# Second attention's opening: own projection of batch 0 in two banks, step 1 in the order of the steps without keys, sums of expert results one step later

## The chip, the cores and the metric

One core of a Trainium2 chip. Its engines run in parallel, each its own program in order, and meet only at semaphores: PE (TensorE: matrix products, into the eight banks of PSUM), DVE (VectorE), ACT (ScalarE), POOL (GpSimd) and SP (SyncE, which here issues transfers). The metric is the device time of one execution in microseconds.

## The reference, cut to what matters

Two layers, each an attention to a context and a mixture of experts. What the change touches is the second attention, which starts while the sums of the first mixture's results are still being added to x.

```python
x = x + tanh(g_ffn[0]) * L0_ffn(layernorm(x))          # 8 experts, top 2: the sums of expert results
x = x + tanh(g_xattn[1]) * L1_xattn(layernorm(x), ctx) # the attention of this change

# L1_xattn, per batch (16 batches, 100 rows, 256 columns, 16 heads of 16), context of 361 rows:
q, k, v    = split(x @ Wqkv + bqkv)
_, ka, va  = split(ctx @ Wqkv_aux + bqkv_aux)
h_main = softmax(q @ k.T / 4)  @ v      # own rows
h_aux  = softmax(q @ ka.T / 4) @ va     # context rows
out    = (h_main * (1 - sigmoid(g)) + h_aux * sigmoid(g)) @ Wo + bo
```

## The kernel before

The function `attend1` holds the second attention: five programs, one for each engine, written out in order. They run over steps t from -1 to 19. In step t the batches t+1 (scores for the maxima), t (exponents), t-1 (sums with the values) and t-2 (output) are under way at once, and the projections of batch t+2 are made.

The scores are computed twice. `by_query(b, u)` puts queries on partitions; DVE's `maxima(b, u)` reduces them to row maxima in two halves. `by_key(b, u)` puts keys on partitions, subtracts the maxima by a further product, and ACT's `exponents(b, u)` reads them. The unit u runs over four: two groups of heads by two members, for `by_query`, and four tiles of keys (own rows, three chunks of the context), for `by_key`. PE alternates: `by_query(t+1, u)`, `by_key(t, u)`, u = 0 to 3. All share three pairs of banks (`scores_free`), so that each product waits for the reader of the one before the last: `by_key(t, u)` for the first half of `maxima(t+1, u)`, `by_query(t+1, u+1)` for the first half of `exponents(t, u)`.

All other products of a step go through the last two banks in turn, in the order of the list `ring`, which is built from `ORDER`, or for the steps 12 to 14 from `LIGHT_ORDER` (the last batches' keys are made by then, so these steps have no key projection; they make the values early and order some of their work differently: the sums over the context in two halves around `by_query(t+1, 2)`, `project_own` behind `by_key(t, 2)`, `values_own` ahead of `by_key(t, 3)`, on ACT `exponents(t, 2)` ahead of `take_own`). `into(name, b)` waits until the bank's last content is taken.

`project_own(b)` makes queries and own keys of batch b: eight products into one bank. ACT's `take_own(b)` copies them: four copies of the queries (each group of heads, masked for two members, `qz`), two of the keys (`kT`). `turn_x(b)` transposes the normalized rows that DVE's `normed(b)` writes; `moments(g)` and `newton(g)` make the statistics of a group of batches (group 0: batches 0 and 1, group 1: 2 and 3, then four each), with a power on POOL between them (`root(g)`). `keep_warm(bank, n)` runs n products whose result nobody reads; these fillers stand in step -1 and 0.

The opening: batches 0 and 1 are transposed and projected, then step -1 makes the four `by_query` of batch 0 with the two key projections of batch 4 between them. In step 0 there is nothing to sum yet. In step 1 the values of batch 2 have been made in advance, so that this step makes keys but no values.

`fed` holds the sums of the first mixture's results. SP loads them back (`fed.ways`), DVE adds the first batches at once (`vector_first`) and then three batches of each group of four (`fed.vector(dve, g)`: six instructions, line 2122); the fourth is weighted by ACT (`fed.scalar`, line 2130) and added by POOL (`fed.gpsimd`, line 2104). Group 1's stand ahead of step -1, group 2's in step 0, group 3's at the end of step 1. `moments(g)` waits for the group it needs.

Behind the last of them the semaphores of the first mixture are handed on to the second: DVE, ACT, PE and SP `leave`, POOL clears them (`second.clear`), and the engines `enter` at the start of step 3 (SP: in its step 2, ahead of `prep.load`, which loads the router and the shared expert of the second mixture).

Lines of the profile: 1392 is `by_query`, 1412 and 1418 `by_key`, 1359 a key projection, 1374 `project_own`, 1366 `turn_x`, 1351 `turn_max` (the transposed maxima, for `take_max` on DVE, line 1094), 1346 a filler, 1434 the sums with the values, 1449 values and output. On DVE 1087 and 1088 are `maxima`, 1051 to 1059 `moments`, 1066 to 1072 `newton`, 1077 `normed`; on ACT 1238 and 1240 are `take_own`, 1249 `exponents`.

## Time and profile before

| | us |
|---|---|
| median of 3 runs | 1229.87 (1229.16 to 1230.22) |
| profiled execution | 1233.03 |
| its span | 1231.3 |
| PE busy | 1169.8 (95%), granted clock 0.98 on average |
| DVE, ACT, POOL busy | 595.4, 479.4, 391.7 |
| second attention, from the own projection to by_query(4,0) | 545.88 to 632.36 |

Times within the trace are us from the start of its span. A row of an engine gives start, busy time, engine, line, operation, what it writes and reads, and in brackets how long the engine had been idle and what ended that.
### The profile page before, as it was taken

What the parts mean: (1) busy time and instruction counts of PE and PEld (TensorE: products, weight loads), DVE (VectorE), ACT (ScalarE), POOL (GpSimd) and SP (SyncE); (2) the same over time, 40 slices, a digit from 0 to 9 for tenths busy, and PEclk for the clock granted to TensorE, in tenths of its full rate; (3) what the DMA queues carried; (4) which work ended last, traced back from release to release, by engine and by line L of the source; (5) the groups of instructions that cost most, each with busy time, mean ns of one, the idle gap of its engine ahead of it and who ended that gap; (6) DMA issues with size and microseconds to landing.
All of it is one profiled execution on the core that took longest, in us unless ns stands there. A gap on an engine that the chain in (4) does not pass through costs nothing. (4 is left out here: it accounts for less than half of the span.)

```text
span 1231.3 us, 29193 instructions
## 1 busy us (share of the span) xinstructions
PE 1169.8 (95%) x11425; PEld 901.6 (73%) x11425; DVE 595.4 (48%) x1437; ACT 479.4 (39%) x1130; POOL 391.7 (32%) x411
## 2 busy tenths in 40 slices
PE   6999999977999999998799999999998999999998
PEld 4767777756999999974466666666665579999975
DVE  5777777774210001057566666567656612111226
ACT  3545555523323332324445444444454232233221
POOL 3666666632223222131101011010011245555420
PEclk9999999977999999999899999999999999999999
DMA  6011111305999998640021000000000459999965
GB/s 182 24 28 36 28 37 44 122 15 190 383 325 337 316 341 315 250 135 19 2 87 30 16 21 21 26 9 9 2 9 14 165 196 349 350 360 353 341 224 168
DMA packets 64392, 180.93 MB, mean 147 GB/s; under 512 B 10176, under 2 KB 36608, under 8 KB 55808
## 3 DMA queue, kind: packets, MB, share of 16 engines
q1 hardware_dynamic: 55088, 156.40, 36.9%
q0 software_dynamic: 8064, 22.03, 5.0%
q8 instruction: 92, 1.51, 0.5%
q10 hardware_dynamic: 1104, 0.64, 0.2%
q14 instruction: 44, 0.36, 0.1%
HBM read 163.11 MB, written 15.93 MB: 145 GB/s over the span
## 5 line engine op out<-in xcount | busy, mean ns | idle before, releaser
L2301 ACT ACTIVATE ex_hT<-kept_psum,ex_w 128x128 f32<-128x128 f32 x464 | 132.9, 369 | 294.8 <-PE kept_psum L2356 157.4
L2356 PE MATMUL kept_psum<-ex_xT,ex_w 128*128 128x128 f32 x1856 | 222.5, 276 | 0.0
L2356 PEld LDWEIGHTS kept_psum<-ex_xT,ex_w 128*128 128x128 f32 x1856 | 215.7, 193 | 0.1
L2367 PE MATMUL kept_psum<-ex_w,ex_hT 128*128 128x256 f32 x928 | 214.0, 379 | 0.0
L2263 DVE TENSOR_TENSOR ex_yt<-kept_psum,ex_b 128x256 f32<-128x256 f32 x84 | 35.7, 425 | 353.6 <-PE kept_psum L2367 353.6
L2367 PEld LDWEIGHTS kept_psum<-ex_w,ex_hT 128*128 128x128 f32 x928 | 170.1, 190 | 19.8
L2229 POOL DMA_INDIRECT ex_results<-ex_yt,ex_to_row x84 | 83.0, 988 | 254.9 <-DVE ex_yt L2263 254.9
L1249 ACT ACTIVATE at_probs<-kept_psum 120x800 f32<-120x800 f32 (+2 forms) x128 | 101.3, 842 | 85.5 <-PE kept_psum L1418 85.5
L1088 DVE TENSOR_REDUCE at_negmax<-kept_psum 100x2 f32<-100x722 f32 x128 | 115.5, 902 | 0.0
L568 ACT ACTIVATE at_probs<-kept_psum 120x800 f32<-120x800 f32 (+1 forms) x96 | 80.1, 837 | 73.7 <-PE kept_psum L691 73.6
L410 DVE TENSOR_REDUCE at_negmax<-kept_psum 120x8 bf16<-120x800 f32 (+1 forms) x96 | 90.6, 985 | 23.4 <-PE kept_psum L682 23.0
L329 POOL TENSOR_TENSOR at_sum<-at_probs 120x800 f32<-120x800 f32 (+1 forms) x47 | 76.9, 1635 | 75.1 <-ACT at_probs L568 74.9
L2222 POOL DMA_INDIRECT ex_xt<-ex_normed,ex_from_row x84 | 81.8, 974 | 50.6 <-DVE ex_from_row L1959 25.5
L1779 POOL TENSOR_TENSOR ex_r<-ex_var,kept_mhalf 100x2 f32<-100x2 f32 x16 | 11.3, 705 | 242.1 <-DVE ex_var L1774 242.1
L1087 DVE TENSOR_REDUCE at_negmax<-kept_psum 100x2 f32<-100x200 f32 x128 | 46.4, 363 | 83.6 <-PE kept_psum L1392 83.0
L1392 PE MATMUL kept_psum<-at_kT,at_qz 32*100 32x461 f32 x512 | 68.5, 605 | 5.5 <-ACT at_probs L1249 3.6
L1412 PE MATMUL kept_psum<-at_qz,at_kT 32*120 32x200 f32 (+2 forms) x1024 | 61.5, 354 | 9.7 <-DVE at_negmax L1088 9.2
L1412 PEld LDWEIGHTS kept_psum<-at_qz,at_kT 32*120 32x120 f32 (+2 forms) x1024 | 41.7, 175 | 26.0 <-issue 21.5
L691 PE MATMUL kept_psum<-at_negmax,at_identb 120*120 120x400 bf16 (+1 forms) x192 | 50.7, 347 | 7.6 <-DVE at_negmax L410 7.6
L639 PE MATMUL kept_psum<-at_ctx,at_wk 128*128 128x361 f32 x128 | 48.6, 506 | 7.1 <-DMA at_bk<-in_L_xattn_bk 6.4
L1449 PE MATMUL kept_psum<-at_wkv_aux,at_ctx 128*120 128x256 f32 (+1 forms) x192 | 48.3, 390 | 0.9 <-DVE ex_yt L2263 0.9
L682 PE MATMUL kept_psum<-at_qz,at_kT 32*120 32x200 f32 (+1 forms) x768 | 47.3, 361 | 1.4 <-ACT at_qz L559 0.7
(252 smaller groups left out, 1691.1 us busy)
## 6 DMA issues: line engine op xcount, KB each, us to landing
ex_w<-in_pack_in SPq DMA_DIRECT2D x32, 1028.0 KB
ex_w<-in_pack_out SPq DMA_DIRECT2D x32, 1024.0 KB
ex_w<-in_pack_in SPq DMA_DIRECT2D x52, 514.0 KB
ex_w<-in_pack_out SPq DMA_DIRECT2D x52, 512.0 KB
at_ctx<-in_ctxT SPq DMA_DIRECT2D x31, 361.0 KB, 3.6
ex_normed<-ex_xhat SPq DMA_DIRECT2D x16, 200.0 KB
ex_w<-ex_results SPq DMA_DIRECT2D x6, 400.0 KB
ex_sw<-in_L_ffn_sW SPq DMA_DIRECT2D x2, 1024.0 KB
```

What stands on the lines that cost most here:

```text
L329: pool.tensor_tensor(sum2[0:r, :, :], p[:, :, 0:T2], p[:, :, T2:T], ALU.add).then_inc(sum2_done, 1)
L410: dve.tensor_reduce(negmax[0:r, half, :].rearrange("p (s h) -> p s h", h=HS), by_head, AX, ALU.max, negate=True).then_inc(max_done, 1)
L568: act.activation(probs[t % 2][0:r, j, half * HH:(half + 1) * HH, :].rearrange("p (s h) t -> p s (h t)", s=2), score_pair(t, j, half)[0:r, ...
L1088: dve.tensor_reduce(by_strip[:, :, HS + u], pair[0:T, :, T:KEYS], AX, ALU.max, negate=True).then_inc(max_done, 1)
L1249: act.activation(probs[b % 2][0:r, u, half * HH:(half + 1) * HH, :].rearrange("p (s h) t -> p s (h t)", s=2), score_pair("k", b, u, half)[ ...
L1392: last = pe.matmul(score_pair("q", b, u, strip // 2)[0:T, strip % 2, 0:KEYS], qz[b % NQ][rows, i, a, :], kT[b % NK][rows, i, :], start=Tru ...
L1412: pe.matmul(score_pair("k", b, u, strip // 2)[0:r, strip % 2, i * 2 * T:(i + 1) * 2 * T], kT[b % NK][rows, i, k0:k0 + r], qz[b % NQ][rows, ...
L2222: pool.indirect_dma_start(xt[t % GATHERS][:, :], None, xhd, bass.IndirectOffsetOnAxis(from_row[:, t:t + 1], 0)).then_inc(gathered[t % GATH ...
L2229: pool.indirect_dma_start(ways, bass.IndirectOffsetOnAxis(to_row[:, t:t + 1], 0), yt[t % SCATTERS][:, :], None).then_inc(scattered[t % SCA ...
L2301: last = act.activation(hT[t % N][:, c, :], ps_h[:, (t * U + u) % N, i * P:(i + 1) * P], ACT.Gelu, bias=w1[t % N][:, B1 + c:B1 + c + 1])
L2356: last = pe.matmul(ps_h[:, (t * U + u) % N, i * P:(i + 1) * P], w1[t % N][:, c * ff + f:c * ff + f + P], xT[t % N][:, c, :], start=(c == 0 ...
L2367: last = pe.matmul(ps_y[:, t % N, 0:D], hT[t % N][:, c, :], w2[t % N][:, c * D:(c + 1) * D], start=(c == 0), stop=(c == FC - 1))
```

## The change

- The own projection of batch 0 goes into two banks (`own`, `own_more`), each with one group of heads, queries and keys. ACT's `take_first_own` copies the first bank, waits for its own copies, then the second; `by_query(0, u)` waits for the copy of its own queries only (`first_own_taken`). `project_own(1)` moves behind `by_query(0, 0)`.
- In step -1 the key projections of batch 4 move down by one unit; four fillers stand behind `by_query(0, 3)`, and five new ones behind `turn_max(0)` in step 0.
- Step 1 takes `NO_VALUES_ORDER`: keys as before, and the rest in the order of the steps without keys.
- The DVE sums of group 1 go from ahead of step -1 into step 0, those of group 2 from step 0 into step 1 and those of group 3 from the end of step 1 into step 2, between the first two maxima there. `moments(1)` goes into step 0, `newton(1)` and `normed(2)` behind the second maxima of step 0. POOL makes all its additions ahead of `root(1)`.
- The handover of the semaphores comes one step later on all engines.
- The two buffers `probs` change places, and in the second mixture the tiles `w1` and `b2` move ahead of `shT`.

```diff
...
     mix = m.sb("mix", [T, D])
-    probs = [m.sb(f"probs{i}", [P, UNITS, H, T]) for i in range(2)]
+    probs = [m.sb(f"probs{i}", [P, UNITS, H, T]) for i in (1, 0)][::-1]
     vm = [m.sb(f"vm{i}", [T, H, 32]) for i in range(2)]
...
                    ("turn_aux", -2), ("own", 2), ("mixT", -2), ("value_own", 0), ("out", -2))
-    LIGHT = range(B - NK + 1, B - 1)
+    NO_VALUES_ORDER = (("max", 0), ("key0", 4), ("key1", 4)) + LIGHT_ORDER[3:]
+    LIGHT, NO_VALUES = range(B - NK + 1, B - 1), range(1, 2)
+
+    def order(t):
+        return LIGHT_ORDER if t in LIGHT else NO_VALUES_ORDER if t in NO_VALUES else ORDER
+
+    def spread_out(t):
+        return t in LIGHT or t in NO_VALUES
+
+    first_own_taken = m.sem("first_own_taken")
     ready = {n: m.sem(f"{n}_ready") for n, _ in ORDER}
     taken = {n: m.sem(f"{n}_taken") for n, _ in ORDER}
+    ready["own_more"], taken["own_more"] = m.sem("own_more_ready"), m.sem("own_more_taken")
     x_ready = taken["out"]
...
 
-    opening = [(n, b) for b in range(PRE) for n in ("value01", "value2")] + [(n, b) for n in ("xT", "own") for b in range(2)]
-    ring = opening + [(n, used(n, off, t)) for t in STEPS for n, off in (LIGHT_ORDER if t in LIGHT else ORDER) if used(n, off, t) is not None]
+    opening = [(n, b) for b in range(PRE) for n in ("value01", "value2")] + [("xT", 0), ("xT", 1), ("own", 0), ("own_more", 0), ("own", 1)]
+    ring = opening + [(n, used(n, off, t)) for t in STEPS for n, off in order(t) if used(n, off, t) is not None]
     ring_at = {use: i for i, use in enumerate(ring)}
...
                 early.load_context(sp, t + NC)
-            if t == 2:
+            if t == 3:
                 fed.finished(sp)
...
         root(0)
-        fed.gpsimd(pool, 0)
+        for g in range(NG):
+            fed.gpsimd(pool, g)
         root(1)
-        for g in range(1, NG):
-            fed.gpsimd(pool, g)
         for b in range(B + 4):
-            if b == 2:
+            if b == 3:
                 second.clear(pool)
...
         take_value2(PRE)
-        moments(1)
-        fed.vector(dve, 1)
         for t in STEPS:
...
                 dve.wait_ge(filled, 6 + 2 * NV)
-            if t == 3:
+            if t == 4:
                 second.enter(dve)
...
             if t == 0:
+                moments(1)
+            if t == 1:
+                fed.vector(dve, 2)
+            if t == 2:
+                fed.vector(dve, 3)
+                fed.finished(dve)
+            if on(t + 1):
+                maxima(t + 1, 1)
+            if t == 0:
                 newton(1)
                 normed(2)
-            if on(t + 1):
-                maxima(t + 1, 1)
             if on(t - 2):
...
             if t == 0:
-                fed.vector(dve, 2)
+                fed.vector(dve, 1)
             if t in (1, 2):
...
                 take_value2(t + 1)
-            if t in LIGHT:
+            if spread_out(t):
                 take_value_own(t)
...
                 residual(t - 2)
-            if on(t) and t not in LIGHT:
+            if on(t) and not spread_out(t):
                 take_value_own(t)
-            if t == 1:
-                fed.vector(dve, 3)
-                fed.finished(dve)
+            if t == 2:
                 second.leave(dve)
...
             last.then_inc(taken["own"], 1)
+
+        def take_first_own():
+            act.wait_ge(masks_set, 4)
+            for i, name in enumerate(("own", "own_more")):
+                act.wait_ge(ready[name], 1)
+                bank = ring_bank(name, 0)
+                act.activation(kT[0][:, i, 0:T], bank[:, (KC + i) * T:(KC + i + 1) * T], ACT.Identity, bias=bqk[:, KC + i:KC + i + 1])
+                for a in range(2):
+                    last = act.activation(qz[0][:, i, a, :], bank[:, i * T:(i + 1) * T], ACT.Identity, bias=bqm[:, i, a:a + 1],
+                                          scale=own[:, a:a + 1]).then_inc(first_own_taken, 1)
+                act.wait_ge(first_own_taken, 2 * i + 2)
+                act.sem_inc(taken[name], 1)
 
...
         take_xT(1)
-        take_own(0)
+        take_first_own()
         fed.scalar(act, 1)
...
         for t in STEPS:
-            if t == 3:
+            if t == 4:
                 second.enter(act)
...
                 take_sum(t - 1, 1)
-            if x_batch(t) is not None and t not in LIGHT:
+            if x_batch(t) is not None and not spread_out(t):
                 take_own(x_batch(t))
...
                 exponents(t, 2)
-            if x_batch(t) is not None and t in LIGHT:
+            if x_batch(t) is not None and spread_out(t):
                 take_own(x_batch(t))
-            if t == 3:
+            if t == 4:
                 prep.scale_bias(act)
...
 
+        def project_first_own():
+            pe.wait_ge(taken["xT"], 1)
+            for i, name in enumerate(("own", "own_more")):
+                bank = into(name, 0)
+                for part in (i, KC + i):
+                    for c in range(KC):
+                        last = pe.matmul(bank[:, part * T:(part + 1) * T], w[:, c, part * P:(part + 1) * P], xT[0][:, c, :],
+                                         start=(c == 0), stop=(c == KC - 1))
+                last.then_inc(ready[name], 1)
+
         def by_query(b, u):
             scores_free("q", b, u)
+            if b == 0:
+                pe.wait_ge(first_own_taken, u + 1)
             if u == 0:
-                pe.wait_ge(taken["own"], b + 1)
+                if b > 0:
+                    pe.wait_ge(taken["own"], b + 1)
                 if b < KEYED:
...
         pe.wait_ge(w_loaded, 32)
-        project_own(0)
-        project_own(1)
-        keep_warm(psum[:, 2, :], 2)
+        project_first_own()
         for t in STEPS:
-            if t == 3:
+            if t == 4:
                 second.enter(pe)
...
                 by_query(t + 1, 0)
+            if t == -1:
+                project_own(1)
             if t == 0:
                 turn_max(t)
-            if key_batch(t) is not None:
+                keep_warm(into("xT", 2), 5)
+            if key_batch(t) is not None and t != -1:
                 project_key(key_batch(t), 0)
...
             if t == -1:
-                project_key(key_batch(t), 1)
+                project_key(key_batch(t), 0)
             if on(t - 1):
...
             if on(t - 1):
-                sum_up(t - 1, 1, range(HG // 2 if t in LIGHT else HG))
+                sum_up(t - 1, 1, range(HG // 2 if spread_out(t) else HG))
             if t == 0:
...
                 by_query(t + 1, 2)
-            if t in LIGHT:
+            if spread_out(t):
                 sum_up(t - 1, 1, range(HG // 2, HG))
...
                 prep.early_tensor(pe, range(t - B, t - B + 1))
-            if x_batch(t) is not None and t not in LIGHT:
+            if x_batch(t) is not None and not spread_out(t):
                 project_own(x_batch(t))
...
                 by_key(t, 2)
-            if x_batch(t) is not None and t in LIGHT:
+            if x_batch(t) is not None and spread_out(t):
                 project_own(x_batch(t))
...
             if t == -1:
-                keep_warm(into("max", 0), 3)
+                project_key(key_batch(t), 1)
             if t == 0:
...
                 by_query(t + 1, 3)
+            if t == -1:
+                keep_warm(into("max", 0), 4)
             if t == 0:
...
                 values2(t + 1)
-            if t in LIGHT:
+            if spread_out(t):
                 values_own(t)
...
                 project_out(t - 2)
-            if on(t) and t not in LIGHT:
+            if on(t) and not spread_out(t):
                 values_own(t)
...
             addend = m.sb("addend", [T, GB, D])
+            b2s = m.sb("b2", [P, E, D])[:, :, :]
+            w1 = [m.sb(f"w1_{i}", [P, B1 + FC]) for i in range(N)]
             shT = [m.sb(f"shT{i}", [P, FS, GT]) for i in range(2)]
-            b2s = m.sb("b2", [P, E, D])[:, :, :]
             syT = Pool(nc, "ex1", scaled_at).sb("syT", [P, KC, GT])
...
         yt = [m.sb(f"yt{i}", [P, D]) for i in range(SCATTERS)]
-        w1, w2 = slots("w1_", [P, B1 + FC]), slots("w2_", [P, FC * D])
+        if not shared:
+            w1 = slots("w1_", [P, B1 + FC])
+        w2 = slots("w2_", [P, FC * D])
         if shared:
```

## Rows read from the trace of the kernel before

**Rows 1.** One stretch: its length, busy us of PE, PEld, DVE, ACT, POOL, granted clock, DMA
```profile
600.00:610.00 10.00, 6.33 (x37) 3.59 (x37) 6.69 (x14) 2.13 (x3) 0.00 (x0) 0.75 0.00 0
```

**Rows 2.** PE in order of time: start us, busy us, line, operation, idle time, releaser
```profile
545.88 3.79 PE L1374 MATMUL kept_psum<-at_xT,at_wqkv 128*128 128x100 f32 x32 [0.20 <-ACT at_xT L1228]
...
550.06 1.03 PE L1392 MATMUL kept_psum<-at_kT,at_qz 32*100 32x461 f32 x8
551.02 1.48 PE L1359 MATMUL kept_psum<-at_ctx,at_wkv_aux 128*128 128x361 f32 x4
...
560.83 0.28 PE L1351 MATMUL kept_psum<-kept_ident,at_negmax 100*128 100x100 f32 x1
562.96 0.94 PE L1412 MATMUL kept_psum<-at_qz,at_kT 32*100 32x200 f32 x16 [1.85 <-DVE at_negmax L1088]
...
565.57 1.88 PE L1392 MATMUL kept_psum<-at_kT,at_qz 32*100 32x461 f32 x8
...
569.89 0.39 PE L1366 MATMUL kept_psum<-kept_ident,at_xhat 100*128 100x100 f32 x2
...
570.98 1.03 PE L1392 MATMUL kept_psum<-at_kT,at_qz 32*100 32x461 f32 x8
...
590.05 2.28 PE L1434 MATMUL kept_psum<-at_probs,at_va 121*32 121x100 f32 x96
...
598.05 1.87 PE L1392 MATMUL kept_psum<-at_kT,at_qz 32*100 32x461 f32 x8 [1.74 <-ACT at_probs L1249]
601.31 1.71 PE L1412 MATMUL kept_psum<-at_qz,at_kT 32*120 32x200 f32 x16 [1.39 <-DVE at_negmax L1088]
...
603.28 1.90 PE L1449 MATMUL kept_psum<-at_wqkv,at_xT 128*100 128x256 f32 x4
...
605.20 1.03 PE L1392 MATMUL kept_psum<-at_kT,at_qz 32*100 32x461 f32 x8
...
610.26 0.94 PE L1412 MATMUL kept_psum<-at_qz,at_kT 32*100 32x200 f32 x16 [2.62 <-DVE at_negmax L1088]
...
632.36 1.03 PE L1392 MATMUL kept_psum<-at_kT,at_qz 32*100 32x461 f32 x8
...
655.25 1.03 PE L1392 MATMUL kept_psum<-at_kT,at_qz 32*100 32x461 f32 x8
```

**Rows 3.** ACT in order of time: copies of batch 0's own projection, exponents in step 1
```profile
547.91 1.42 ACT L1238 ACTIVATE at_qz<-kept_psum,at_bqm,at_own 128x100 f32<-128x100 f32 x4 [1.86 <-PE kept_psum L1374]
549.21 0.59 ACT L1240 ACTIVATE at_kT<-kept_psum,at_bqk 128x100 f32<-128x100 f32 x2
...
597.04 1.59 ACT L1249 ACTIVATE at_probs<-kept_psum 120x800 f32<-120x800 f32 x2
```

**Rows 4.** DVE in order of time, from the opening to step 2
```profile
546.08 0.74 DVE L1051 BATCH_NORM_STATS2 at_stats<-kept_x 100x6 f32<-100x256 f32 x2
...
547.22 2.65 DVE L2122 SCALAR_TENSOR_TENSOR kept_x<-ex_ways,ex_gates,kept_x 100x256 f32<-100x256 f32 x6
551.23 0.37 DVE L1087 TENSOR_REDUCE at_negmax<-kept_psum 100x2 f32<-100x200 f32 x1 [1.36 <-PE kept_psum L1392]
...
553.57 0.37 DVE L1087 TENSOR_REDUCE at_negmax<-kept_psum 100x2 f32<-100x200 f32 x1
...
563.81 0.15 DVE L1066 TENSOR_TENSOR at_newt<-at_r 100x2 f32<-100x2 f32 x1
...
564.60 0.41 DVE L1077 TENSOR_SCALAR at_xhat<-kept_x,at_mv,at_rstd 100x256 f32<-100x256 f32 x1
...
587.35 0.37 DVE L1087 TENSOR_REDUCE at_negmax<-kept_psum 100x2 f32<-100x200 f32 x1 [2.60 <-PE kept_psum L1392]
...
605.56 2.65 DVE L2122 SCALAR_TENSOR_TENSOR kept_x<-ex_xhat,ex_gates,kept_x 100x256 f32<-100x256 f32 x6
```

**Rows 5.** POOL in order of time: its last additions of expert results
```profile
555.99 3.14 POOL L2104 TENSOR_TENSOR kept_x<-kept_x,ex_weighted 100x256 f32<-100x256 f32 x4 [4.12 <-ACT ex_weighted L2130]
```

**Rows 6.** SP's queue in order of time: the first load behind the handover
```profile
614.14 0.37 SPq L1737 DMA_DIRECT2D ex_router<-in_L_ffn_gW  x1
```

## The prediction

> **What bounds the kernel now.** The core's PE is the long engine; the question is only what the opening of the second attention (545 to 655 us of the trace) costs beyond a settled step. I read first the stretches of 10 us: between 600 and 610 us PE is busy for 6.33 us at a granted clock of 0.75, where a PE that sets the end should be busy throughout at 1.00 [rows 1]. Then PE's instructions in order of time. A settled step, from by_query(4,0) to by_query(5,0), takes 655.25 - 632.36 = 22.89 us; step 2, from 605.20 to 632.36, takes 27.16 us for the same work, so 4.3 us of it are opening [rows 2]. In steps 0 and 1 the reader is to see four waits of PE: 1.85 us before by_key(0,0), 1.74 before by_query(2,3), 1.39 before by_key(1,3), 2.62 before by_key(2,0) [rows 2]. Each is the end of a chain between PE, DVE's maxima and ACT's exponents. The third thing is the clock: a by_query of 1.03 us took 1.88 at 565.57 [rows 2]. That is the lower of the two levels, 1.2 instead of 2.4 GHz, and it comes each time just behind one of those waits.
>
> **Own projection of batch 0.** Before, all 8 products of batch 0 and the 8 of batch 1 run in one go (32 passes, 3.79 us from 545.88), ACT then makes 4 + 2 copies of batch 0, and by_query(0,0) starts at 550.06 [rows 2, 3]. After, the first bank holds 4 products: 3.79/4 = 0.95, done at 546.83. ACT starts 0.13 later (as it starts at 547.91 for 16 passes that end at 547.78), makes one key copy (0.59/2 = 0.30) and one query copy (1.42/4 = 0.36); with 0.2 for the semaphore that is 547.8 [rows 3]. PE is through the second bank then too, so by_query(0,0) starts at 547.85: **2.2 earlier**. DVE's maxima start 1.17 behind it (551.23 for 550.06), at 549.0 [rows 2, 4]. DVE is free for that only because the expert sums that ended at 547.22 + 2.65 = 549.87 go to step 0; had they stayed, 0.85 would be lost again [rows 4].
>
> The added wait on ACT for its own two copies stands before the second half, the sum of ways 1 and batch 1's copies. by_query(1,0) needs the last of them at 558, they are due at 552.8: no cost while these 5 us last; I bound it by 0 to 0.3 us (one copy).
>
> In step -1 DVE sets the pace: 553.57 - 551.23 = 2.34 per unit of scores, the first half of it after 1.17, PE 0.15 later [rows 4]. But project_own(1), 1.90 us, now lies between by_query(0,0) and (0,1) where one key product of 1.48 lay [rows 2]: by_query(0,1) starts at 547.85 + 0.96 + 1.90 = 550.7 and its maxima at 551.9 where DVE alone would be ready at 551.35. The key products, moved down by one unit, then fit (0.96 + 1.48 = 2.44 against a unit of 2.5): units at 553.2 and 555.7, last maxima 556.9 to 559.2, turn_max(0) at 559.3 instead of 560.83. **Of the 2.2, 1.5 is left** [rows 2].
>
> **Step 0.** From turn_max(0) to by_key(0,0) DVE takes 562.96 - 560.83 = 2.13, to 561.45; five fillers lie in PE's wait of 1.85. by_key takes 1.1 (0.94 and the shift passes), half an exponent 0.8 (1.59/2), semaphores 0.25: by_query(1,1) at 563.6 where before it began at 565.57, behind fillers at the low clock, and took 1.88 instead of 1.03 [rows 2, 3]. So 2.8 are won at its end, and given back: moments(1) (547.22 - 546.08 = 1.14) lies in DVE's idle time before maxima(1,1) at 564.8, but newton(1) and normed(2) (563.81 to 565.01, 1.2) now come behind these maxima, at 567.05, and turn_x(2), which did not wait before, waits for xhat of batch 2 until 568.4, 1.2 us of idle PE [rows 4]. With 570.98 - 569.89 = 1.09 of transposes and fillers by_query(1,2) starts at 569.5, before 570.98 [rows 2]. fed.vector(1), 2.65, follows on DVE until 570.9; by_query(1,2)'s maxima could start at 570.7, and PE is in project_own(2) until 572.4 (3.79/2 = 1.9), while by_key(0,2) is released at 572.2: hidden, and up to 0.5 us more if that cover fails. The root that POOL owes for newton(1) now comes after its additions, the last of which ends at 559.1, before its input is there at 563.6; it has until 567 [rows 5]. **The lead stays 1.5.**
>
> **Step 1**, in the times of before. fed.vector(2) now lies between maxima(2,0) and (2,1): 2.65 into an idle time of 2.60, nothing [rows 4]. The sums over the context (2.28 from 590.05) are cut in two, by_query(2,2) goes between, at 591.2; its first maxima are ready at 593.5, by_key(1,2) runs from 593.65 to 594.75, project_own(3) to 596.65 [rows 2]. ACT now takes the exponents ahead of take_own(3), which had held them up to 597.04 and so PE to 598.05: half of them is done at 595.65, by_query(2,3) starts when PE is free, at 596.6, at the full clock [rows 2, 3]. values_own(1) (1.90 at half the clock, so 0.95) fills the wait for its maxima; by_key(1,3) at 599.1 instead of 601.31. Then a new wait: nothing is left behind by_key(1,3), and by_query(3,0) waits for its exponents (1.1 + 0.8 + 0.25): 601.26 instead of 605.20. **3.9 gained.**
>
> **Step 2.** fed.vector(3) no longer stands ahead of take_max(2) (605.56 to 608.2), so the 2.62 us before by_key(2,0) go [rows 2, 4]. It now stands between maxima(3,0) and (3,1): by the settled step by_query(3,1) comes 4.9 after by_query(3,0), its maxima can start at 6.05, and DVE is through maxima(3,0) at 3.45 and the sums at 6.1: I take 0.1. The step then takes 22.89 + 0.1 = 23.0 for 27.16. **4.2 gained.** The bound if that cover is missing is 2.65.
>
> **Other moves.** The handover of semaphores moves from step 2 to 3: SP, which waited at 614.14 for it, 5.9 behind DVE's last sum at 608.2, would issue the shared weights some 6 us after step 2's end, 17 us ahead of step 4, the first to wait for it [rows 6]. Behind SP's wait stand load_context(9) and the weights; both are used a step or more later. The swapped buffers and the 4 more fillers cost nothing beyond what is counted.
>
> **Sum.** 1.5 + 3.9 + 4.2 = 9.6 us. The profiled execution is 1233.03 us, 1231.3 its span, the median of the runs 1229.87. PE is busy all through later steps, so an earlier by_query(4,0) (622.8 for 632.36) shifts the rest, and I take the sum from the median: **1220.3 us**. The bounds of the terms (0.5 to 2.2, 2.5 to 4.3, 1.5 to 4.3) give 1219 to 1225.4.
>
> **Rivals.** (a) *The clock falls again.* Behind a wait of 1.39 to 1.85 it fell; the new order leaves 0.6 and 1.2 close together before turn_x(2), and 0.6 and 0.75 around by_key(1,3) [rows 2]. One stretch at 1.2 GHz costs two by_query at 0.85 each, 1.7: 1222; two 1223.7. Chance 0.22. The page "TensorE: Matmul & The Clock Gate" of the Trainium skill (Part 1) says that how many matmuls run slow differs from run to run of one kernel. The three runs lie within 1.06 us, less than one such stretch, so this trace speaks against it here; by the page the gain would scatter by that much.
> (b) *The expert sums are not covered.* One of the three calls of 2.65 us shows on PE, as fed.vector(3) did before: 1223. For it speaks that covers (2) and (3) are exact to 0.1. Chance 0.12.
> (c) *The opening gives nothing*, as DVE's maxima bind in step -1 whatever PE does: 1221.8. Against it: DVE idled 1.36 us for by_query(0,0) [rows 4]. Chance 0.08.
> (d) *The stalls come back elsewhere*: DVE and ACT answer by the same latencies, and each closed wait opens at the next exponent; all of steps 1 and 2 but the moved 1.5 is lost, 1228.4. Chance 0.06.
> (e) *Slower, by the clock.* The 1.2 GHz level holds from step 0 to step 2. Each us of PE work in it costs nearly one (0.85 for 1.03). It decides from some 12 us of PE work at that level, beyond which the 9.6 and 0.2% are eaten; with 16 us the time is 1220.3 + 0.85 x 16 = 1234. Against it: at 605 us the clock was back after one busy stretch, by_query(3,0) at 1.03 [rows 2]. Chance 0.04.
>
> **How the numbers follow.** 1220.3 has the remaining chance of 0.48. The range from 1218.0 (half of the waits that I added in step 0 vanish, and the fillers cost less) to 1225.5 (bounds above, rivals a, b and c) leaves out d and e and some of the tails, about 0.16. This kernel's measurement tells 0.2%, 2.5 us, from no change: faster means below 1227.4. Faster 0.88, same 0.07 (d and part of e), slower 0.05.
>
> **What would show it.** Right: by_query(0,0) 2.2 us behind the start of the own projection instead of 4.2; turn_max(0) 13.4 behind it; clock 1.00 in all stretches from 560 to 620; no wait over 1.3 us on PE, the longest ahead of turn_x(2); exponents ahead of take_own(3); no idle PE ahead of by_key(2,0) but 0.1; by_query(4,0) 77 us behind the own projection instead of 86.5. Wrong: a clock below 1, DVE's sums named as releaser of PE, or a later PE wait for the handover.

## The result, and the profile after

The changed kernel takes 1222.92 us (median; 1221.97 to 1227.95), the kernel before, measured beside it again, 1231.18. The ratio is 0.994, 95% interval 0.9926 to 0.9954: 7.4 us gained, 5.7 to 9.1 (the two medians differ by 8.26). A second series gave 0.9943 (0.9925 to 0.996). The forecast was 1220.3 us and a gain of 9.6. The span of the profiled execution fell from 1231.3 to 1220.3 us, but that pair overstates it, as the runs below show.

Two of the stretches of 10 us of the changed kernel (columns as in [rows 1]):

```profile
560.00:570.00 10.00, 8.24 (x88) 5.77 (x80) 8.56 (x25) 3.36 (x5) 1.40 (x2) 1.00 0.00 0
...
600.00:610.00 10.00, 9.73 (x197) 6.29 (x198) 8.22 (x24) 5.34 (x9) 0.00 (x0) 1.00 0.01 3
```

PE is busy for 9.73 us between 600 and 610 where it was for 6.33 at a clock of 0.75 [rows 1], and the clock is 1.00 in each stretch of the opening. PE in order of time:

```profile
544.08 2.00 PE L1407 MATMUL kept_psum<-at_xT,at_wqkv 128*128 128x100 f32 x16 [0.19 <-ACT at_xT L1240]
546.20 1.03 PE L1429 MATMUL kept_psum<-at_kT,at_qz 32*100 32x461 f32 x8
547.16 2.03 PE L1398 MATMUL kept_psum<-at_xT,at_wqkv 128*128 128x100 f32 x16
...
557.41 0.28 PE L1375 MATMUL kept_psum<-kept_ident,at_negmax 100*128 100x100 f32 x1
...
559.53 0.94 PE L1449 MATMUL kept_psum<-at_qz,at_kT 32*100 32x200 f32 x16 [0.71 <-DVE at_negmax L1097]
...
561.66 1.03 PE L1429 MATMUL kept_psum<-at_kT,at_qz 32*100 32x461 f32 x8 [0.16 <-ACT at_probs L1273]
...
566.28 0.36 PE L1390 MATMUL kept_psum<-kept_ident,at_xhat 100*128 100x100 f32 x2 [1.08 <-DVE at_xhat L1086]
...
567.27 1.03 PE L1429 MATMUL kept_psum<-at_kT,at_qz 32*100 32x461 f32 x8
...
592.95 1.03 PE L1429 MATMUL kept_psum<-at_kT,at_qz 32*100 32x461 f32 x8
...
595.38 0.95 PE L1449 MATMUL kept_psum<-at_qz,at_kT 32*120 32x200 f32 x16 [0.36 <-DVE at_negmax L1097]
...
597.48 1.03 PE L1429 MATMUL kept_psum<-at_kT,at_qz 32*100 32x461 f32 x8 [0.73 <-ACT at_probs L1273]
...
599.90 0.94 PE L1449 MATMUL kept_psum<-at_qz,at_kT 32*100 32x200 f32 x16
...
620.45 1.03 PE L1429 MATMUL kept_psum<-at_kT,at_qz 32*100 32x461 f32 x8
...
636.53 1.99 PE L1486 MATMUL kept_psum<-at_wkv_aux,at_ctx 128*121 128x256 f32 x8 [0.52 <-issue]
```

Line 1429 is by_query, 1449 by_key, 1375 turn_max, 1390 turn_x, 1407 and 1398 the own projections, 1486 values and output. by_query(0,0) starts 546.20 - 544.08 = 2.12 us behind the own projection (4.18 before, [rows 2]), turn_max(0) 13.33 behind it (14.95 before), by_query(4,0), at 620.45, 76.37 (86.48 before). The last row stands in step 3; the part on why the prediction was right or wrong comes back to it. The waits of 1.74 and 2.62 us of [rows 2] are gone, that of 1.39 is 0.36. That of 1.85 ahead of by_key(0,0) shows as 0.71, since five fillers now stand in it. Two are new: 1.08 ahead of turn_x(2) and 0.73 ahead of by_query(3,0). ACT and DVE, in order of time:

```profile
545.28 0.34 ACT L1260 ACTIVATE at_kT<-kept_psum,at_bqk 128x100 f32<-128x100 f32 x1 [1.02 <-PE kept_psum L1407]
545.52 0.75 ACT L1262 ACTIVATE at_qz<-kept_psum,at_bqm,at_own 128x100 f32<-128x100 f32 x2
...
591.10 1.57 ACT L1273 ACTIVATE at_probs<-kept_psum 120x800 f32<-120x800 f32 x2 [0.81 <-PE kept_psum L1455]
593.06 1.41 ACT L1250 ACTIVATE at_qz<-kept_psum,at_bqm,at_own 128x100 f32<-128x100 f32 x4 [0.39 <-PE kept_psum L1398]
```

```profile
547.37 0.37 DVE L1096 TENSOR_REDUCE at_negmax<-kept_psum 100x2 f32<-100x200 f32 x1 [3.00 <-PE kept_psum L1429]
...
580.94 2.65 DVE L2165 SCALAR_TENSOR_TENSOR kept_x<-ex_xhat,ex_gates,kept_x 100x256 f32<-100x256 f32 x6
583.63 0.37 DVE L1096 TENSOR_REDUCE at_negmax<-kept_psum 100x2 f32<-100x200 f32 x1
...
600.76 2.65 DVE L2165 SCALAR_TENSOR_TENSOR kept_x<-ex_xhat,ex_gates,kept_x 100x256 f32<-100x256 f32 x6
603.55 0.37 DVE L1096 TENSOR_REDUCE at_negmax<-kept_psum 100x2 f32<-100x200 f32 x1
```

ACT copies one key part and two query parts as soon as the first bank is there, and in step 1 the exponents (591.10) come ahead of take_own(3) (593.06), the other way round than in [rows 3]. On DVE the maxima follow the sums of expert results (2.65 us each, line 2165): at 583.63 no wait is shown where [rows 4] had 2.60 (587.35), and none at 603.55. The first load behind the handover on SP:

```profile
626.35 0.37 SPq L1777 DMA_DIRECT2D ex_router<-in_L_ffn_gW  x1
```

That is in step 3, 17.6 us ahead of PE's step 4 (by_query(5,0), at 643.92), the first that waits for the handover.

In the table the places are us behind the start of the own projection, read from PE's rows in each kernel's trace. The last of them, by_query(4,0), is called the opening. The last column names the steps in which PE's granted clock stood at 0.50 for a while, which is called a stretch at 1.2 GHz here.

| kernel | turn_max(0) | turn_max(1) | by_query(3,0) | by_query(4,0) | low clock |
|---|---|---|---|---|---|
| before | 14.95 | 35.31 | 59.32 | 86.48 | steps 0, 1, 2 |
| before, second trace | 14.96 | 35.11 | 58.84 | 84.27 | steps 0, 1 |
| before, third trace | 14.96 | 36.21 | 57.67 | 84.83 | steps 0, 2 |
| before, places of the tiles changed | 14.96 | 36.21 | 60.04 | 85.53 | steps 0, 1 |
| after, four traces | 13.33 | 33.39 | 53.40 | 76.37 | none |
| own projection alone | 13.43 | 33.80 | 56.72 | 82.16 | steps 0, 1 |
| step 1's order alone | 14.96 | 35.17 | 55.18 | 79.42 | step 0 |
| sums alone | 14.96 | 36.36 | 59.45 | 82.43 | steps 0, 1 |
| after without fillers | 13.33 | 36.84 | 56.85 | 79.82 | step 0 |
| after, both sums in step 2 | 13.32 | 34.95 | 54.96 | 80.39 | step 0 |
| further version | 13.33 | 31.28 | 52.11 | 75.08 | none |

### The profile page after: what moved, and what is told of

The parts are those of the page before. It is cut to its first block and busy times, and to the rows that moved or that the text cites. A ratio compares the mean times of both kernels' runs of the same rounds, so it can differ in the third digit from the quotient of the medians.

```text
span 1220.3 us, 29213 instructions
## 1 busy us (share of the span) xinstructions
PE 1164.6 (95%) x11433; PEld 899.5 (74%) x11433; DVE 596.4 (49%) x1437; ACT 478.2 (39%) x1130; POOL 390.7 (32%) x411
```

## The experiments

**The kernel before, again** (r_before, r_before2). No edit. Two traces, to see what of the opening belongs to the order and what to the run.

> The kernel before once more, unchanged, for a second trace of its opening. The opening (start of the own projection to by_query(4,0)) was 86.5 us in the first trace. If its three stretches at 1.2 GHz belong to its waits, they come again behind the same waits and the opening is 86 to 87 us. If their place is a matter of chance from run to run, the opening differs by 1.5 us or more. Time within 0.2% of before by either.

> The kernel before, a third trace. In the first two its opening was 86.5 and 84.3 us: the stretch at 1.2 GHz in step 0 came in both, the one in step 1 in two lengths, the one in step 2 only in the first. If the stretches' place is a matter of chance, this opening lies anywhere between 83.5 and 86.5, with step 2 near 25.6. If the first trace is the rule, it is 86.5 with step 2 at 27.2.

Measured: openings of 84.27 and 84.83 us; the time of the first was 0.9999 of before (0.9987 to 1.001). PE's rows of the second trace and then of the third, by_query (line 1392) and by_key (1412):

```profile
597.35 1.40 PE L1392 MATMUL kept_psum<-at_kT,at_qz 32*100 32x461 f32 x8 [1.74 <-ACT at_probs L1249]
...
609.21 0.94 PE L1412 MATMUL kept_psum<-at_qz,at_kT 32*100 32x200 f32 x16 [2.32 <-DVE at_negmax L1088]
```

```profile
596.49 1.03 PE L1392 MATMUL kept_psum<-at_kT,at_qz 32*100 32x461 f32 x8 [1.74 <-ACT at_probs L1249]
598.91 0.95 PE L1412 MATMUL kept_psum<-at_qz,at_kT 32*120 32x200 f32 x16 [1.39 <-DVE at_negmax L1088]
...
606.15 0.94 PE L1412 MATMUL kept_psum<-at_qz,at_kT 32*100 32x200 f32 x16 [2.62 <-DVE at_negmax L1088]
...
609.73 1.53 PE L1392 MATMUL kept_psum<-at_kT,at_qz 32*100 32x461 f32 x8
```

The waits are nearly the same in all three traces: 1.74, 1.39 (1.38 in the second), 2.62 (2.32 in the second). The clock is not. In the second trace by_query(2,3) takes 1.40 us, nearly half of it slow; in the third 1.03, and step 1, from turn_max(1) to by_query(3,0), takes 57.67 - 36.21 = 21.46 us instead of the 24.0 of the first. Behind the wait of 2.62 the third trace has a slow by_query again (1.53), the second had none. So the waits at the end of step 1 and in step 2 can bring a stretch at 1.2 GHz and need not; behind the wait of 1.85 in step 0 all three traces have one. The first trace, on which the prediction rests, was the only one of three with all of them: 86.48 is the dear end, the mean of the three is 85.2.

**The changed kernel, again** (r_after, r_after2, r_after3). No edit.

> The changed kernel once more, unchanged. Its opening was 76.4 us in the first trace with no stretch at 1.2 GHz. If that is the order's doing it is 76 to 77 us again, 10.1 less than before, and the time 9 to 10 us below before. If the clock falls by chance, one or two stretches show in this trace, the opening is 78 to 80 us, and the time 6 to 8 us below before.

> The changed kernel, a third trace. In the first two the opening was 76.4 us without a stretch at 1.2 GHz; a variant that is the same up to step 2 had one behind the wait of turn_x(2) and took 1.6 us more in step 0. By chance of place: 76.4 in most traces and 78 in some. If the new order excludes such stretches, 76.4.

> The changed kernel, a fourth trace, for the same question: 76.4 us, or 78 with a stretch at 1.2 GHz behind the wait of turn_x(2).

Measured: 76.38, 76.37 and 76.37 us, the four traces alike in every place of the table. The time of the first was 0.9943 of before, 7 us less and not 9 to 10, although no stretch fell into its opening: neither branch of its expectation held whole. Against the mean of before the opening gains 85.2 - 76.4 = 8.8 us, 7.9 to 10.1 by single traces; 8.8 lies within the interval of the time (5.7 to 9.1). Step 3 gives a little back: 23.47, 23.20, 23.20 and 22.88 us in the four traces, 22.88 or 22.89 in all three of before.

**No fillers** (e_nofill).

```diff
-                keep_warm(into("xT", 2), 5)
...
-            if t == 0:
-                keep_warm(into("xT", 2), 3)
...
-            if t == 0:
-                keep_warm(into("own", 2), 3)
...
-                keep_warm(into("max", 0), 4)
...
-                keep_warm(into("value_own", 0), 3)
```

> The changed kernel without any filler from step -1 on (24 products whose result nobody reads). No filler is on the path by the trace, so by the theory that they hold the clock the opening grows from 76.4 to 79 to 82 us, by two or more stretches at 1.2 GHz, each about 1.7 us. If the new order alone keeps the clock up, the opening stays at 76.4 or gets 0.3 shorter.

Measured: opening 79.82, ratio to before 0.9972 (0.9957 to 0.9986). The stretch of step 0 and four of PE's rows in it:

```profile
559.50:572.50 13.00, 9.73 (x65) 5.43 (x65) 9.45 (x26) 3.36 (x5) 1.40 (x2) 0.50 0.01 1
```

```profile
559.91 1.67 PE L1449 MATMUL kept_psum<-at_qz,at_kT 32*100 32x200 f32 x16 [1.85 <-DVE at_negmax L1097]
...
562.93 1.87 PE L1429 MATMUL kept_psum<-at_kT,at_qz 32*100 32x461 f32 x8 [1.02 <-ACT at_probs L1273]
...
569.25 1.88 PE L1429 MATMUL kept_psum<-at_kT,at_qz 32*100 32x461 f32 x8 [0.29 <-ACT at_probs L1273]
571.06 3.02 PE L1398 MATMUL kept_psum<-at_xT,at_wqkv 128*128 128x100 f32 x16
```

Both by_query of step 0 take 1.87 and 1.88 us, project_own(2) 3.02 instead of 2.03, and the clock is at 0.50 for the 13 us of this row. The wait of 1.85 ahead of by_key(0,0), where five fillers stood, is back. The step is 36.84 - 33.39 = 3.45 us longer. No filler shortens anything by its own work, and three even stand on PE's path (between turn_x(2) and by_query(1,2), where the changed kernel shows no idle time). Yet without them 3.45 of the 8.8 us of the opening are lost, and by the time about half of the gain, though the intervals just overlap (0.9957 to 0.9986 here, 0.9925 to 0.996 with them in the same series). So with this order the fillers hold the clock. They are not enough by themselves: the kernel before has 20 fillers too, two of them just ahead of step -1, and its clock falls. What the five new ones behind turn_max(0) would give in the order of before was not run.

**Both sums in step 2** (e_cover).

```diff
-            if t == 1:
-                fed.vector(dve, 2)
             if t == 2:
+                fed.vector(dve, 2)
                 fed.vector(dve, 3)
```

> The changed kernel with the DVE sums of group 2 moved on from step 1 to step 2, beside those of group 3: 5.3 us instead of 2.65 between the first two maxima of step 2. If the cover there is just 2.7 us, by_key(2,1) comes 2.6 us later and the opening is 79.0 us. If DVE has more slack in that step than that, it stays below 77.5. Step 1 should not change, as DVE waited for PE there: if it gets shorter by 0.5 or more, the sums of group 2 were not covered in step 1.

Measured: opening 80.39, ratio to before 0.9977 (0.9963 to 0.9992). DVE in step 2, then PE there (1428 by_query, 1448 by_key):

```profile
606.45 5.21 DVE L2164 SCALAR_TENSOR_TENSOR kept_x<-ex_xhat,ex_gates,kept_x 100x256 f32<-100x256 f32 x12
611.70 0.37 DVE L1096 TENSOR_REDUCE at_negmax<-kept_psum 100x2 f32<-100x200 f32 x1
```

```profile
608.04 1.03 PE L1428 MATMUL kept_psum<-at_kT,at_qz 32*100 32x461 f32 x8
...
613.03 0.95 PE L1448 MATMUL kept_psum<-at_qz,at_kT 32*121 32x200 f32 x16 [2.56 <-DVE at_negmax L1097]
```

DVE is held for 5.21 us, its maxima start at 611.70 instead of some 609.2, and by_key(2,1) waits for 2.56 us. by_query(3,0) to by_query(4,0) takes 25.43 instead of 22.97. So the cover in step 2 is one call of the sums and no more. Step 1, from turn_max(1) to by_query(3,0), is 20.01 us with and without the call in it: there it was hidden. The other 1.56 us of this run are in step 0, which the edit does not touch:

```profile
570.41 0.36 PE L1389 MATMUL kept_psum<-kept_ident,at_xhat 100*128 100x100 f32 x2 [1.08 <-DVE at_xhat L1086]
570.61 1.19 PE L1369 MATMUL kept_psum<-at_wkv_aux,kept_ident 128*128 128x128 f32 x6
571.73 1.87 PE L1428 MATMUL kept_psum<-at_kT,at_qz 32*100 32x461 f32 x8
```

Behind the wait of 1.08 ahead of turn_x(2) (line 1389) the clock fell, fillers and by_query(1,2) at the low level (1.87). It is what rival (a) of the prediction described, in a program that up to there is the changed kernel's. In the four traces of the changed kernel it did not come; one trace of five has it, so the new order does not exclude it.

**Own projection alone** (e_own), on the kernel before: `project_first_own`, `take_first_own` and step -1 as in the change.

```diff
-        project_own(0)
-        project_own(1)
-        keep_warm(psum[:, 2, :], 2)
+        project_first_own()
...
+            if t == -1:
+                project_own(1)
```

> The kernel before with the two-bank own projection of batch 0 alone (and the key projections of step -1 one unit lower, four fillers at its end); sums, step 1 and handover as before. By the sum of the prediction turn_max(0) comes 13.4 us behind the start of the own projection instead of 14.95 (1.5 us less), and the opening is 85.0 us; the sums of group 1 that still stand ahead of step -1 cost nothing more, as project_own(1) sets the second unit. If DVE binds the opening, turn_max(0) is at 14.3 or later and the opening 86 us or more.

Measured: opening 82.16, ratio to before 0.9986 (0.997 to 1.0002). PE at its start (line 1419 by_query, 1365 turn_max, 1439 by_key), then DVE's first maxima:

```profile
548.35 2.00 PE L1397 MATMUL kept_psum<-at_xT,at_wqkv 128*128 128x100 f32 x16 [0.20 <-ACT at_xT L1230]
550.48 1.03 PE L1419 MATMUL kept_psum<-at_kT,at_qz 32*100 32x461 f32 x8
...
561.78 0.28 PE L1365 MATMUL kept_psum<-kept_ident,at_negmax 100*128 100x100 f32 x1
563.90 1.24 PE L1439 MATMUL kept_psum<-at_qz,at_kT 32*100 32x200 f32 x16 [1.85 <-DVE at_negmax L1090]
```

```profile
552.27 0.36 DVE L1089 TENSOR_REDUCE at_negmax<-kept_psum 100x2 f32<-100x200 f32 x1
```

turn_max(0) comes 561.78 - 548.35 = 13.43 us behind the own projection, as the sum had it, although the sums of group 1 still stand ahead of the maxima. They hold the first maxima until 552.27, 1.79 us behind by_query(0,0) where the changed kernel has 1.17, and of these 0.6 us 0.10 is left at turn_max(0). The opening misses the 85.0 expected: the wait of 1.85 stays and the stretches fell shorter and fewer than in the first trace of before. The time does not tell it from before.

**Step 1's order alone** (e_step1), on the kernel before: the list `NO_VALUES_ORDER` and `spread_out(t)` in place of `t in LIGHT`.

```diff
+    LIGHT, NO_VALUES = range(B - NK + 1, B - 1), range(1, 2)
...
-            if x_batch(t) is not None and t in LIGHT:
+            if x_batch(t) is not None and spread_out(t):
                 take_own(x_batch(t))
```

> The kernel before with step 1 in the order of the steps without keys alone. By the theory step 1 (turn_max(1) to by_query(3,0)) falls from 24.0 to 20.1 us and step 2 also gets shorter, as take_max(2) stands behind less: its wait before by_key(2,0) falls from 2.6 to 1.2 us and one stretch at 1.2 GHz goes: opening 79 to 81 us. If step 1's gain is given back in step 2, the opening is 82.5 us or more.

Measured: ratio 0.9957 (0.9943 to 0.997), opening 79.42. PE at the end of step 1 and in step 2 (1400 by_query, 1420 by_key):

```profile
597.99 1.03 PE L1400 MATMUL kept_psum<-at_kT,at_qz 32*100 32x461 f32 x8
...
602.52 1.03 PE L1400 MATMUL kept_psum<-at_kT,at_qz 32*100 32x461 f32 x8 [0.73 <-ACT at_probs L1257]
...
606.32 0.94 PE L1420 MATMUL kept_psum<-at_qz,at_kT 32*100 32x200 f32 x16 [1.35 <-DVE at_negmax L1096]
```

Step 1, up to by_query(3,0), takes 55.18 - 35.17 = 20.01 us. The new wait of 0.73 is there, and by_key(2,0) waits for 1.35 instead of 2.62: DVE now starts the sums of group 3 0.91 us ahead of by_query(3,0) (601.61 and 602.52) and not 0.36 behind it (605.56 and 605.20, [rows 2, 4]). No stretch at 1.2 GHz falls into steps 1 and 2. By the time this is the largest of the three parts.

**Sums alone** (e_sums), on the kernel before: the calls of `fed.vector`, `moments(1)`, `newton(1)`, the handover and the places of the tiles as in the change.

```diff
-            if t == 1:
-                fed.vector(dve, 3)
-                fed.finished(dve)
-                second.leave(dve)
+            if t == 2:
+                second.leave(dve)
```

> The kernel before with the sums of expert results and the handover one step later alone (moments(1) and newton(1) moved with them). By the theory the wait of 2.62 us before by_key(2,0) and the stretch at 1.2 GHz behind it go, step 2 falls from 27.2 to 23.0 us, and step 0 loses up to 1.2 us by the wait for xhat of batch 2: opening 82.3 to 83.5 us. If DVE's sums show up elsewhere, step 2 stays above 25 us.

Measured: opening 82.43, ratio 0.9986 (0.9972 to 1.0001). PE in step 0 (1368 turn_x), then in step 2 (1394 by_query, 1414 by_key):

```profile
572.23 0.36 PE L1368 MATMUL kept_psum<-kept_ident,at_xhat 100*128 100x100 f32 x2 [1.07 <-DVE at_xhat L1076]
```

```profile
606.50 1.03 PE L1394 MATMUL kept_psum<-at_kT,at_qz 32*100 32x461 f32 x8
...
608.93 0.94 PE L1414 MATMUL kept_psum<-at_qz,at_kT 32*100 32x200 f32 x16
```

turn_x(2) waits for 1.07 us, as foreseen, and step 0 takes 21.40 us where the three traces of before took 20.36, 20.15 and 21.25. by_key(2,0) no longer waits, and step 2 takes 82.43 - 59.45 = 22.98 us. Taken alone the moved sums win 2.5 us or more in step 2 and pay up to 1.2 of them in step 0. The time does not tell the run from before.

**The places of the tiles alone** (e_place), on the kernel before: `probs` swapped, `b2` and `w1` ahead of `shT`.

> The kernel before with the places of the tiles alone changed (the two probs swapped, b2 and w1 ahead of shT), the program otherwise the same. From the last turn_max on, the kernels with the old places took 327.0 to 327.2 us in four traces, those with the new ones 327.4 to 327.5 in six. If the places make that difference, this run takes 327.4 or more there; if the moved sums or handover do, 327.0 to 327.2.

Measured: 327.86 us from the last turn_max on, the most of all fourteen traces, in a single execution of 1231.11 us. But the third trace of before, with the old places, took 327.63 there: the two groups overlap, and the seeming gap of 0.3 us was no rule. A cost of a few tenths by the places is neither shown nor excluded. The opening, 85.53 us, is one more of the order of before.

**Further** (v_spread).

```diff
+        moments(1)
         for t in STEPS:
...
+    LIGHT, NO_VALUES = range(B - NK + 1, B - 1), range(0, 2)
...
             if t == 0:
-                moments(1)
+                newton(1)
+                normed(2)
...
+            if t == 0:
+                keep_warm(into("own", 2), 4)
             if on(t):
                 by_key(t, 2)
```

> The changed kernel, further: moments(1) goes back ahead of step -1, where DVE waited 3.0 us, newton(1) and normed(2) ahead of the second maxima of step 0, so that turn_x(2) no longer waits (1.08 us in the first trace); and step 0 takes the order that step 1 got (exponents ahead of take_own(2), project_own(2) behind by_key(0,2), values_own(0) ahead of by_key(0,3)), which should take the 0.87 us wait before by_query(1,3). Opening 76.4 - 1.1 - 1.1 = 74.2 us if both hold; 75.3 if only the first does; 76.4 or more if the waits move to the next exponent.

Measured: opening 75.08 us, ratio to before 0.9926 (0.9905 to 0.9948), median 1221.71. PE in steps 0 and 1 (1389 turn_x, 1428 by_query, 1448 by_key):

```profile
567.36 0.39 PE L1389 MATMUL kept_psum<-kept_ident,at_xhat 100*128 100x100 f32 x2
...
571.05 0.95 PE L1448 MATMUL kept_psum<-at_qz,at_kT 32*120 32x200 f32 x16 [0.48 <-DVE at_negmax L1097]
...
574.06 1.03 PE L1428 MATMUL kept_psum<-at_kT,at_qz 32*100 32x461 f32 x8
...
578.59 1.03 PE L1428 MATMUL kept_psum<-at_kT,at_qz 32*100 32x461 f32 x8 [0.73 <-ACT at_probs L1272]
```

Besides what is shown, the two groups of three fillers around by_query(1,3) go, and the four new ones stand ahead of by_key(0,2). turn_x(2) no longer waits, and by_query(1,3) at 574.06 follows PE's own work without the 0.87: turn_max(1) comes 31.28 us behind the own projection instead of 33.39, 2.1 gained as expected. Then by_query(2,0) waits for 0.73 for exponents, since nothing is left to do behind by_key(0,3), and of the 2.1 only 75.08 to 76.37, 1.3, are left. It is the same give-back as at the end of step 1. By its trace this version is ahead of the changed kernel; by the time, whose intervals overlap, that is not settled.

## Why the prediction was right or wrong

- **What bounds the opening**: right. Of the four waits that it named (the last of them, 2.62, stands in step 2 and not in step 1) 1.74 and 2.62 went, 1.39 fell to 0.36, and 1.85 was filled with five fillers, 0.71 left. By its places on PE the changed kernel followed the sum to 0.6 us (76.4 for 77).
- **Own projection**: right. by_query(0,0) stands 2.12 us behind the own projection where the sum gives 547.85 - 545.88 = 1.97 (the "2.2 us behind" under "What would show it" is the gain, put in the wrong place); it gains 4.18 - 2.12 = 2.06 for 2.2. turn_max(0) is at 13.33 for 13.4. Rival (c) fell with e_own. One reason was wrong: with the sums left ahead of step -1, 0.85 us were to be lost again, and e_own lost 0.10.
- **Step 0**: the wait ahead of turn_x(2) was forecast as 1.2 and is 1.08; turn_max(1) came 20.06 us behind turn_max(0), 20.36 before. What pays for the new wait is the clock: with a stretch at 1.2 GHz in it (e_cover) the new step 0 took 21.63. The sum took the stretch of before as gone, with rival (a) for its return, and did not say that this hangs on the five fillers behind turn_max(0); by e_nofill and by the table at the end the step keeps its clock only with them.
- **Step 1**: the times after are right (by_query(2,3) without a wait, the new wait of 0.73 at its end, by_query(3,0) at 53.4 for 53.9). The gain of 3.9 was mis-sized. The third trace of before had no stretch at 1.2 GHz in this step and took 21.46 us; against the 20.01 after, the order is worth 1.45. The rest of the 3.9, some 2.5 us, was the clock in the first trace.
- **Step 2**: the time after is right (22.97 for 23.0), and e_cover shows that the cover of the sums is as thin as the sum said, so rival (b) held for a second call and not for the first. The gain of 4.2 was mis-sized in the same way: without a stretch behind the wait before took 25.43 us (second trace), so the moved sums are worth 2.5 and the other 1.7 were one stretch.
- **The term that was mis-sized** is the base of the sum: "I take the sum from the median", with the three stretches of one trace as if every run paid them. With the stretch of step 0 alone, which every trace of before has, the terms are 1.6 + 0.3 + 1.45 + 2.5 = 5.85 us; with all stretches 10.1. Runs of before pay some of them, and 7.4 measured lies between. The 9.6 forecast lies outside the interval of the gain, 5.7 to 9.1. The forecast time is 2.6 us below the median measured; half of that is the base, which was 1231.18 when measured again and not 1229.87.
- **Rival (a)**: the prediction said that its trace and three times within 1.06 us spoke against stretches that differ from run to run. That was wrong: three traces of one kernel have them in steps 0, 1 and 2, in steps 0 and 1, and in steps 0 and 2. The three times lay close by luck: seven runs of before spread from 1229.16 to 1234.68 us, and the profiled execution, 1233.03, was already 2.8 above the highest of the three. The page "TensorE: Matmul & The Clock Gate" (Part 1) of the Trainium skill says that the same kernel has a different number of slow matmuls at its start from run to run. The three traces show the like in the middle of a kernel.
- **Slower, by the clock** (e): it did not come. But e_nofill shows its mechanism, 13 us at the low level in step 0, as soon as the fillers are gone; the step lost 3.45 us by it, where 9.6 and the 2.5 of 0.2% had to be lost. By the price that the rival used, 0.85 us lost for each us of PE's work, that takes (9.6 + 2.5)/0.85 = 14 us and not 12.
- **Handover and other moves**: the handover was off the path, as said. Step 3 took 0.3 to 0.6 us more in three of four traces of the changed kernel, and 22.88 in the fourth. The traces show where: PE stood idle for 0.52 us (0.25 in two others) ahead of the values of step 3 (line 1486, 636.53), and the profile names no engine as the end of it, only "issue". e_cover, e_nofill and v_spread have the same handover and took 22.88, e_sums 23.20. What makes the gap stays open.

## What to carry to other kernels

Where PE waits in short pieces, price the clock apart from the waits: take the same stretch from several traces, and count a slow stretch as a chance and not as a rule. A new order is worth what its waits are worth at the full clock, plus part of the stretches that go with them. Work that is moved under a cover should be held against that cover's length: one call of 2.65 us was free where a second one cost 2.46.

## What the runs showed that was not expected

- Counted over all fourteen traces, the stretches at 1.2 GHz go with the waits, and each place has its own chance:

| idle time of PE | traces with it | of these with a stretch there | traces without it | of these with a stretch there |
|---|---|---|---|---|
| 1.85 us ahead of by_key(0,0), step 0 | 8 | 8 | 6 (five fillers in it) | 1 (e_cover, later in the step) |
| 1.74 and 1.4 us at the end of step 1 | 6 | 5 | 8 | 0 |
| 2.3 to 2.6 us in step 2 | 6 | 2 | 8 | 0 |

- The own projection started at 542.6 to 548.4 us in kernels whose PE program up to there is the same (fourteen traces), a spread of nearly 6 us. Part of it is the clock in the first layer: up to 540 us the mean granted clock was 0.98 in the traces that started at 542.63, 543.42 and 544.28, and 0.97 in the other eleven (544.08 to 548.35). Two spans of single executions can differ by nearly as much as this change is worth; places counted from a common start agreed to 0.01 us in the four traces of the changed kernel, up to by_query(4,0).
- The parts, each on the kernel before, moved the time by 0.9986, 0.9957 and 0.9986, together 0.993; the whole by 0.994. They add up within their intervals. By the openings of single traces they come to 3.0, 5.8 and 2.8 us, 11.6 against 8.8 for the whole: step 1's order and the moved sums both shorten the wait of 2.62 us, and that counts 1.3 of them twice (2.62 - 1.35); where the rest lies single traces do not tell.
- The clock fell where no wait was longer than 1.85 us (step 0 of all three traces of before, with 0.52 and 1.34 us idle just ahead of it, in step -1), and in e_cover behind waits of 0.71, 0.53 and 1.08 us.
